# Keys and first rows loaded first and turned on TensorE, later keys in two buffers and three steps ahead

## The reference

```python
x = x + tanh(g_xattn) * softmax(layernorm(x) @ keys.T) @ keys
x = x + tanh(g_ffn) * (layernorm(x) @ W.T + bias)     # W = mean(|weight|) per output row * sign(weight)
```

## Time and profile before

| | |
|---|---|
| median of 3 runs | 1171.01 us (1170.32 to 1174.28) |
| profiled execution | 1170.11 us, span 1168.3 us |
| TensorE matmul busy | 1041.8 us, 89% |
| VectorE busy | 761.7 us, 65% |
| ScalarE, GpSimd busy | 347.5 us, 230.7 us |
| mean granted TensorE clock | 0.963 |
| TensorE busy in 0 to 50, 50 to 100, 100 to 150, 150 to 200 us | 6.84, 18.87, 37.59, 44.08 us |
| TensorE busy in 400 to 450 us | 50.00 us |

### The profile page before, as it was taken

How to read it: one execution, slowest core, us unless ns; L and a number is a source line. 1 busy time by engine, 2 the same in 40 slices (tenths; PEclk the granted TensorE clock), 3 DMA queues, 4 the chain that set the end, 5 groups by cost and what they waited for, 6 DMA issues and landing times.

```text
span 1168.3 us, 14014 instructions
## 1 busy us (share of the span) xinstructions
PE 1041.8 (89%) x5680; PEld 511.3 (44%) x5680; DVE 761.7 (65%) x1072; ACT 347.5 (30%) x278; POOL 230.7 (20%) x301
## 2 busy tenths in 40 slices
PE   0325968899979999999889999999799999999998
PEld 0313534344434444444444444444344444444443
DVE  3536868676676776676586667766586666677531
ACT  1723755222222222222232222222132222222100
POOL 0004110122221112222222211122222221113100
PEclk9966989899989999999989999999999999999999
DMA  8769471785556555556645655555745565553221
GB/s 261 169 111 193 148 180 37 184 213 139 136 140 141 119 127 118 144 145 144 157 114 144 145 139 118 127 122 144 181 114 131 134 145 144 127 126 73 72 77 68
DMA packets 287776, 159.25 MB, mean 136 GB/s; under 512 B 276448, under 2 KB 276448, under 8 KB 276960
## 3 DMA queue, kind: packets, MB, share of 16 engines
q1 hardware_dynamic: 285408, 141.58, 52.1%
q10 hardware_dynamic: 2304, 16.78, 4.6%
HBM read 55.58 MB, written 33.55 MB: 76 GB/s over the span
## 4 chain that ended last, share of the span: by engine, by line
PE 75%; issue 11%; DVE 5%; DMA 3%; POOL 2%; SPq 2%; ACT 1%; ACTq 0%; POOLq 0%; DVEq 0%
PE y_ps L808 66%; PE s_ps L778 4%; PE c_ps L793 4%; DMA xn<-in_ctx_dram 3%; SPq L274 1%; POOL xr L360 1%; DVE x1n L561 1%; DVE kmax L613 1%; SPq L266 0%; DMA xr<-in_x_dram 0%; DVE xr L591 0%; DVE prob L581 0%; DVE qn L556 0%; ACT xn L407 0%; DVE st L549 0%
## 5 line engine op out<-in xcount | busy, mean ns | idle before, releaser
L808 PE MATMUL y_ps<-wsign,x1t 128*128 128x512 fp8e4 x4096 | 924.6, 382 | 16.8 <-DMA x1t<-x1n 13.4
L808 PEld LDWEIGHTS y_ps<-wsign,x1t 128*128 128x128 f16 x4096 | 400.7, 99 | 496.4 <-issue 23.5
L420 ACT ACTIVATE xn<-xr,nm,r 128x2048 f32<-128x2048 f32 x32 | 67.0, 2092 | 352.6 <-POOL nm L353 350.8
L591 DVE SCALAR_TENSOR_TENSOR xr<-c_ps,coef,xr 128x512 f32<-128x512 f32 x128 | 95.7, 747 | 98.2 <-PE c_ps L793 98.2
L603 DVE TENSOR_TENSOR ytmp<-y_ps,alpha_b 128x512 f32<-128x512 f32 x128 | 86.2, 673 | 101.2 <-PE y_ps L808 101.2
L360 POOL TENSOR_TENSOR xr<-xr,bias_b 128x2048 f32<-128x2048 f32 x32 | 144.5, 4516 | 4.4 <-ACT xn L420 4.4
L561 DVE SCALAR_TENSOR_TENSOR x1n<-xn,x1n 128x2048 f16<-128x2048 f32 x32 | 132.7, 4147 | 12.3 <-ACT x1n L426 12.3
L793 PE MATMUL c_ps<-kd,pt 128*128 128x512 f16 x256 | 79.9, 397 | 32.3 <-DVE xr L591 31.4
L345 POOL TENSOR_TENSOR ve<-mv,eps 128x1 f32<-128x1 f32 x32 | 8.0, 250 | 498.3 <-DVE mv L598 498.3
L607 DVE TENSOR_TENSOR xr<-ytmp,xr 128x512 f32<-128x512 f32 x128 | 97.2, 759 | 4.4
L594 DVE BATCH_NORM_STATS2 st<-xr 128x6 f32<-128x512 f32 x128 | 88.9, 694 | 4.4
(11 more groups left out here) (61 smaller groups left out, 348.3 us busy)
## 6 DMA issues: line engine op xcount, KB each, us to landing
xr<-in_x_dram SPq DMA_DIRECT2D x32, 1024.0 KB, 6.9
out_dram<-xr SPq DMA_DIRECT2D x31, 1024.0 KB, 4.8
xr<-n_L_ffn_weight_real_dram ACTq DMA_DIRECT2D x8, 1024.0 KB, 6.2
spare<-n_L_ffn_weight_real_dram ACTq DMA_DIRECT2D x8, 1024.0 KB, 4.9
xn<-in_ctx_dram SPq DMA_DIRECT2D x8, 512.0 KB, 6.6
qt<-qn SPq DMA_TRANSPOSE x64, 4.7
...
x1t<-x1n SPq DMA_TRANSPOSE x64, 5.1
```

Source lines behind the costliest of these rows:

```text
L420: nc.scalar.activation(xn2[:, :], xr[:, u % RX, :], ACT.Identity, bias=nm2[:, :], scale=r2[:, :]).then_inc(xn2_set, 1)
L591: nc.vector.scalar_tensor_tensor(out=xr[:, r, chunk(n)], in0=c_ps[:, n % 2, :], scalar=coef[:, 0:1], in1=xr[:, r, chunk(n)], op0=ALU.mult, ...
L808: last = nc.tensor.matmul(y_ps[:, bank_y(t, n), :], x1t[:, t % RT, part, block(k)], wsign[:, k, chunk(n)], start=(k == 0 and part == 0), s ...
```

## The change

- **SP.** Keys 0, tiles 0 and 1 are loaded first, the gates behind them; ACT starts to load weights when tile 0 is in. Keys 0 and rows of tile 0 (query and x1) are no longer turned by DMA.
- **TensorE** turns keys 0, the query rows of tile 0 and the x1 rows of tile 0 (`turn_rows`), eight transposes at a time through the two banks of the weights; ACT and VectorE copy them out (`take_keys`, `take_q`, `take_x1`). `PAIRS` lists the order in which weights, keys and rows use the banks, and `pair_tr`, `out_act`, `out_dve` count it.
- **Key maximum of batch 0**: spread, one TensorE transpose and a VectorE maximum in place of POOL's reduction.
- **Rows.** For tile 0 (query) and tiles 0 and 1 (x1) ACT writes the high part straight from `xr`, and VectorE makes the normalised rows itself (`rows_q`, `rows_x1`). The factor 2^10 moves into the rstd, so the low part is a plain subtraction.
- **Later keys**: `kd` and `kt` get a second buffer (in `spare` and `sg`), keys are loaded into `spare`, and the step of batch b is 8b - 5 (tiles 3, 11, 19) instead of 8b - 3.
- **Tables** of the 48 blocks shift by one to three places, absolute sums of weights 0 to 3 go to ACT; statistics and query of tile 5 leave the 48 blocks for tile 3, where scores, probabilities and attention stand behind blocks 9, 11 and 12 to 15.
- **POOL**: `add_bias` and the power of the rstd wait for `x1_high` (or `q_high`) too.

```diff
-    W_AT = {0: 4, 2: 5, 4: 6, 6: 7, 10: 8, 13: 9, 16: 10, 19: 11, 25: 12, 28: 13, 31: 14, 34: 15}
+    W_AT = {2: 4, 4: 5, 6: 6, 7: 7, 11: 8, 14: 9, 17: 10, 20: 11, 25: 12, 28: 13, 31: 14, 34: 15}
...
+    KEYS_STEP = {TPB * b - 5: b for b in range(1, NB)}
...
+    LATE_SCORES, LATE_PT, LATE_C = 9, 11, {12: 0, 13: 1, 14: 2, 15: 3}
...
+        kts = [kt_even[:, :, :], sg[:, 0, :].rearrange("p (a k) -> p a k", a=ND)]
+        kds = [kd_even[:, :, :], spare[:, 1, :].bitcast(F16).rearrange("p (a n) -> p a n", a=2)]
...
             def load_keys(b):
-                if b > 0:
-                    sp.wait_ge(x1_low, TPB * b - 1)
+                if b == 1:
+                    sp.wait_ge(w_signed, NW)
...
+                elif b > 1:
+                    sp.wait_ge(key_low, b)
...
-            sp.dma_start(gates[:, 0:1], g_xattn.partition_broadcast(P)).then_inc(gates_in, 16)
-            sp.dma_start(gates[:, 1:2], g_ffn.partition_broadcast(P)).then_inc(gates_in, 16)
             load_keys(0)
             load_x(0)
             load_x(1)
-            turn_keys(0)
+            sp.dma_start(gates[:, 0:1], g_xattn.partition_broadcast(P)).then_inc(gates_in, 16)
+            sp.dma_start(gates[:, 1:2], g_ffn.partition_broadcast(P)).then_inc(gates_in, 16)
...
             def add_bias(u):
                 pool.wait_ge(xn2_set, u + 1)
+                pool.wait_ge(x1_high, u + 1)
...
             def high_keys(b):
                 act.wait_ge(ctx_in, 32 * (b + 1))
                 act.wait_ge(kscale_set, b + 1)
-                act.wait_ge(c_ready, TPB * b * NC)
-                act.wait_ge(kt_turned, 32 * b)
+                act.wait_ge(c_ready, TPB * (b - 1) * NC if b > 0 else 0)
...
+            def rows_x1(u):
+                dve.wait_ge(nm2_set, u + 1)
...
+                nc.vector.tensor_scalar(xn2[:, :], xr[:, u % RX, :], r2[:, 0:1], nm2[:, 0:1], ALU.mult,
+                                        ALU.add).then_inc(xn2_set, 1)
...
-                nc.vector.scalar_tensor_tensor(out=x1n[:, 1, :], in0=xn2[:, :], scalar=LN_SCALE, in1=x1n[:, 0, :],
-                                               op0=ALU.mult, op1=ALU.subtract).then_inc(x1_low, 1)
+                nc.vector.tensor_tensor(x1n[:, 1, :], xn2[:, :], x1n[:, 0, :], ALU.subtract).then_inc(x1_low, 1)
...
+            ln1_mean(5)
+            low_x1(4)
+            low_q(5)
+            finish_y(3, 0)
+            ln1_mean(6)
+            finish_y(3, 1)
+            max_logits(5)
+            split_probs(5)
+            low_q(6)
+            finish_y(3, 2)
+            for n in range(NC):
+                attention(5, n)
+            key_scales(1)
+            low_keys(1)
...
+            def turn_rows(kind, u, halves, high, low, g):
+                p = pair(kind, u, g)
+                for part in range(2):
+                    pe.wait_ge(low if part else high, u + 1)
+                    wait_banks(p, part)
+                    for b in range(HALF):
+                        last = nc.tensor.transpose(w_turn[part][:, block(b)], halves[:, part, block(HALF * g + b)],
+                                                   ident16[:, :])
+                    last.then_inc(pair_tr, 1)
```

More of the change, by code:

```diff
@@ L670, in _ @@
             low_keys(0)
-            sum_abs(0)
+            rows_q(0)
             low_q(0)
+            take_keys(0)
+            take_keys(1)
+            take_q(0, 0)
+            take_q(0, 1)
             ln1_mean(1)
-            spread_alpha(0)
+            max_logits(0)
             take_w(0)
-            sum_abs(2)
-            spread_alpha(1)
+            split_probs(0)
+            low_q(1)
             take_w(1)
-            low_q(1)
-            max_logits(0)
-            split_probs(0)
-            spread_alpha(2)
-            take_w(2)
-            take_w(3)
             for n in range(NC):
                 attention(0, n)
+            take_w(2)
+            rows_x1(0)
+            low_x1(0)
+            take_x1(0, 0)
+            take_x1(0, 1)
+            ln1_mean(2)
+            max_logits(1)
+            take_w(3)
+            spread_alpha(0)
+            spread_alpha(1)
+            split_probs(1)
+            spread_alpha(2)
             spread_alpha(3)
-            max_logits(1)
-            ln1_mean(2)
-            split_probs(1)
+            low_q(2)
             take_alpha(0)
-            low_x1(0)
-            for n in range(NC):
+            for n in range(NC - 1):
                 attention(1, n)
-            low_q(2)
             dve.wait_ge(bias_in, 16)
@@ L777, in scores @@
                     for part in range(2):
-                        last = nc.tensor.matmul(s_ps[:, 0:P], qt[:, part, block(k)], kt[:, k, :],
+                        last = nc.tensor.matmul(s_ps[:, 0:P], qt[:, part, block(k)], kts[b % 2][:, k, :],
                                                 start=(k == 0 and part == 0), stop=(k == ND - 1 and part == 1))
@@ L792, in attend @@
                 for part in range(2):
-                    last = nc.tensor.matmul(c_ps[:, n % 2, :], pt[:, :], kd[:, part, chunk(n)],
+                    last = nc.tensor.matmul(c_ps[:, n % 2, :], pt[:, :], kds[u // TPB % 2][:, part, chunk(n)],
                                             start=(part == 0), stop=(part == 1))
```

373 lines of the change are left out of this document (245 added, 128 removed).

## The result

The changed kernel takes 1183.47 us (median of 4 runs, 1182.2 to 1186.69) against 1170.66 for the kernel before: ratio 1.0112, 95% interval 1.0083 to 1.014. It is **slower** by 1.1%, where 1156.5 was forecast. Its profiled execution has a span of 1180.5 us, 12.2 more than before's.

The account below looks back on a forecast made before the run. TensorE was taken to bound the kernel, with time to win at key tiles and the start; -29.0 + 3.0 - 5.1 + 13.5 + 4.0 = -13.6 took 1170.1 to 1156.5 us, range 1138 to 1167.

Parts of the forecast that it names:

- Rival C: First three tiles and tiles 4, 12, 20: VectorE loses to GpSimd's bias adds, 1177 us; chance 0.10 together with D.
- D: Key steps: keys three steps ahead but read too late for another reason, the 29 us stay, 1182 us; chance 0.02.
- All 29.0 us go: Three tiles preparing new keys: TensorE needs the keys three tiles later, so their whole excess vanishes, -29.0 us.
- I take 1.5 for each of tiles 11 and 19 ... +3.0: Tiles 11 and 19: VectorE hands back later after key work, delaying the next tile's maximum and probabilities, +3.0 us.
- +4.0: Tile 4: attention, key work, finish and statistics make probabilities ready at T + 63, TensorE asking at T + 59.
- 4.5, one bias add: Tiles 11 and 19: upper bound for the lateness of one tile, one GpSimd bias add of 4.5 us.
- Tile 3: +13.5: Tile 3: work moved there makes TensorE wait 8 us for the query, scores run slowly, attention steps wait; +13.5 us.
- Start up to the first FFN block: Kernel start: first scores at 31 us, second at 60, first FFN block at 84.5, 11 us early.
- First three tiles ... -5.1: 48 blocks of the first three tiles: most of the start's gain given back, tile 3 beginning at 232.5 against 237.6.
- rival B: First three tiles: start's gain all given back, block 16 at 159 or more, total 1163 us; chance 0.20.
- I take 7: SP's DMA transposes: a transposed pair taken as 7 us, between 5.1 and 9.5.
- The 3.4 us wait for weight 15: Behind block 16 in the first three tiles: TensorE's 3.4 us wait stays, with the same order on VectorE.

Follow-up runs that it names:

- the repairs: Changed kernel with tile 5's statistics and query back among the 48 blocks, later key maxima over TensorE, probabilities split before x1 after key steps: 1148.83 us.
- Experiments 2 and 10: Changed kernel, bias add from tile 2 on without waiting for x1's high part: 1179.01 us; changed kernel, bias add of tiles 5, 13, 21 one column: 1171.1 us.
- Experiment 4: Changed kernel with tile 5's statistics, query and transposes back among the 48 blocks and tile 3 in the order of later tiles: 1168.78 us.

## Why the prediction was wrong

The sign was missed: 13.6 us of gain forecast, 12.2 of loss measured in the span. The difference of 25.8 lies in these terms, in the order of the prediction. That the time falls near rivals C (1177) and D (1182) says nothing for them: D had the keys read too late, and no wait for keys is among the waits; C had most of its loss in the first three tiles, where the splits of x1 of tiles 1 and 2 took 2.29 us and lost no race.

- **"All 29.0 us go": right.** The distances of the old key steps are 31.20, and with the repairs no key step costs more than 0.34 us.
- **"I take 1.5 for each of tiles 11 and 19 ... +3.0", and "+4.0" for tile 4: the step that failed**, by 9.9 and 7.9 us, 17.8 of the 25.8. I had counted the reply of the reduction as 1.2 us with its small operations, and rstd2 behind it as late by no more than VectorE is. VectorE's own lateness was right (logits "0.8 us late", measured 0.86). The term put at nothing is GpSimd's: behind the all-reduce it falls silent for 6.7 to 7.2 us, and in tile 11 rstd2 starts 11.2 us after mean and variance are there, 3.6 of them before the all-reduce and 0.4 in it. The trace of before had the row, in the timeline of GpSimd at the start, and I did not read it:

```profile
19.46 0.38 POOL L364 PARTITION_ALL_REDUCE kmax_all<-kmax  x1 [17.63 <-DVE kmax L613]
...
27.46 0.18 POOL L333 TENSOR_TENSOR ve<-mv,eps 128x1 f32<-128x1 f32 x1 [7.62 <-issue]
```

  In the old key steps the silence lay in idle time, as the attention behind the key maximum had still to run. The change moved the key maximum behind the attention, so that rstd2 was already due. My upper bound "4.5, one bias add" left out that the split itself can be late: it is 4.1 us late, the bias add costs 2.0 more than in a normal tile, and slow matmuls add 1.5.
- **Rival C named the second link** (a bias add that starts with the split, by the new wait, and stops the probabilities), but as a race to be lost by chance, with 0.10 together with D. It was no race: once GpSimd's reply was late, the same event released both. Experiments 2 and 10 price it at 6.5 us for the new wait in three steps and at 3.9, 6.1 and 5.4 us a step for the whole exclusion. Its "Against", that VectorE is mostly at the split first in a normal tile, was a wrong reading of before. There too the bias add is first in most tiles, and the split's mean is 4147 ns where the same split of the query takes 2283; the tile hides it:

```profile
L561 DVE SCALAR_TENSOR_TENSOR x1n<-xn,x1n 128x2048 f16<-128x2048 f32 x32 | 132.7, 4147 | 12.3 <-ACT x1n L426 12.3
```

- **"Tile 3: +13.5": right in sum (13.5) and nearly by parts.** "It stands 8 us" was 7.15, slow scores 3.48, the wait for the third attention step 2.75; the wait of 1 for the fourth did not come, but blocks and attention behind the third ran slowly, 1.8 us in all. Experiment 4 shows by its opposite that it was avoidable.
- **"Start up to the first FFN block": right.** 31, 60 and 84.5 were 30.77, 61.09 and 83.92. The last has some luck in it: over nine traces with the same start it lies between 79.8 and 85.0.
- **"First three tiles ... -5.1": 7.8 us off**, rival B's size. Block 4 was put at 107 and ran at 109.28, block 8 at 125 and 127.81, block 16 at 155 and 159.27, tile 3 at 232.5 and 240.34. At block 4 the mis-sized term is the transposed pair, "I take 7": the pair was issued at 99.17 and TensorE went on at 109.28, 10.1 us, while VectorE's rows_x1 lost its race (5.53 us) as I had assumed. (In tile 3 the 7 was right: issued at 257.97, landed at 264.88.) At block 16 the pair was not what I missed. There I had allowed 10 us, from 145 to 155, and it took 10.1; but VectorE's split of tile 2 ended at 149.22 and not at 145, 2.8 of these 4.2 us being there at block 8 already. Behind block 16 I had 77.5 us and it was 81.1, 3.6 more. "The 3.4 us wait for weight 15" became 4.87, with 1.22, 0.62, 0.35 and 0.78 in small waits beside it, where the kernel before had one of 0.61. What exactly lengthened these was not tried.
